# Low terms of gathered quads and of chunks subtracted tile by tile in a one-core graph layer kernel

## The reference

```
h = xn
for layer in range(6):
    agg = segment_sum(h[src], dst, num_segments=n)     # 100000 rows gathered and summed
    z = (h + agg) @ W1[layer] + b1[layer]
    z = relu(batchnorm(z))
    z = z @ W2[layer] + b2[layer]
    h = batchnorm(z)                                   # relu after all layers but the last
x = x + h + mix(xn)
x = x + ffn(layernorm(x))                              # eight experts, two hidden matmuls each
```

## Time and profile before

| | |
|---|---|
| median of 3 runs | 4800.57 us (4792.5 to 4800.67) |
| profiled execution, its own time | 4799.28 us |
| its span | 4797.5 us |
| TensorE busy | 4435.0 us, 92% |
| GpSimd busy | 3121.9 us, 65% |
| VectorE busy | 3031.1 us, 63% |
| ScalarE busy | 2665.6 us, 56% |
| mean granted TensorE clock | 0.962 of full speed |

### The profile page before, as it was taken

How to read it: one execution, slowest core, us unless ns; L and a number is a source line. 1 busy time by engine, 2 the same in 40 slices (tenths; PEclk the granted TensorE clock), 3 DMA queues, 4 the chain that set the end, 5 groups by cost and what they waited for, 6 DMA issues and landing times.

```text
span 4797.5 us, 67657 instructions
## 1 busy us (share of the span) xinstructions
PE 4435.0 (92%) x18799; PEld 3238.3 (68%) x18799; DVE 3031.1 (63%) x6880; ACT 2665.6 (56%) x3373; POOL 3121.9 (65%) x3415
## 2 busy tenths in 40 slices
PE   4999999899988999899988999889998899999999
PEld 3666788587756777477764777567784856666665
DVE  7788766466664666566665666646565566666666
ACT  5667433565536665466545655366554255555555
POOL 5777764077762777457772777627774077877886
PEclk7999999999999999999998999999999899999999
DMA  6444653255533554255543555335545100000000
GB/s 224 155 157 139 209 155 91 79 167 166 155 98 122 171 167 145 58 189 167 158 125 104 165 166 152 98 123 171 165 144 179 39 10 9 9 8 9 8 8 8
DMA packets 197167, 560.26 MB, mean 117 GB/s; under 512 B 44306, under 2 KB 63228, under 8 KB 196668
## 3 DMA queue, kind: packets, MB, share of 16 engines
q0 software_dynamic: 109728, 299.78, 21.3%
q1 hardware_dynamic: 79676, 227.39, 13.9%
q10 hardware_dynamic: 7392, 28.90, 1.5%
HBM read 481.66 MB, written 74.24 MB: 116 GB/s over the span
## 4 chain that ended last, share of the span: by engine, by line
PE 66%; POOL 10%; issue 9%; DVE 6%; DMA 5%; ACT 3%; ACTq 0%; DVEq 0%; POOLq 0%; SPq 0%
PE bank L998 24%; PE bank L1172 11%; PE bank L1181 6%; PE bank L1074 6%; PE bank L903 5%; POOL BIG L737 5%; POOL G L737 5%; PE bank L900 4%; PE bank L946 3%; PE bank L1027 3%; DMA G<-y_table,idx 2%; DMA BIG<-y_table,idx 2%; ACT Gsp L1250 1%; DVE BIG L1506 1%; DVE onehot L1528 1%
## 5 line engine op out<-in xcount | busy, mean ns | idle before, releaser
L737 POOL DMA_INDIRECT G<-y_table,idx x1416 | 1450.1, 1024 | 989.1 <-DMA y_table<-BIG 504.2
L998 PE MATMUL bank<-Ac,Ych 128*128 128x512 f32 x7644 | 1829.9, 393 | 19.3 <-DVE Ych L1512 19.0
L998 PEld LDWEIGHTS bank<-Ac,Ych 128*128 128x128 f32 x7644 | 1447.4, 189 | 328.3 <-DVE Ych L1512 20.2
L1263 ACT CAST Ac<-BIG 128x2048 fp32r<-128x2048 uint8 (+1 forms) x546 | 912.9, 1687 | 373.1 <-PE bank L903 248.2
L737 POOL DMA_INDIRECT BIG<-y_table,idx x870 | 897.7, 1032 | 265.2 <-issue 251.8
L1528 DVE TENSOR_SCALAR onehot<-iota,rel 128x128 fp32r<-128x128 f32 x2290 | 541.5, 306 | 204.2 <-PE bank L903 175.6
L2007 DVE TENSOR_TENSOR G<-G,bank 128x448 f32<-128x448 f32 x784 | 462.1, 619 | 215.2 <-ACT G L1427 112.1
L903 PE MATMUL bank<-Gsp,onehot 128*128 128x512 f32 x1750 | 514.3, 415 | 20.9 <-DVE Gsp L1519 20.7
L1519 DVE TENSOR_TENSOR Gsp<-G,Gsp 128x1024 fp32r<-128x1024 f32 (+1 forms) x230 | 271.0, 1178 | 351.2 <-ACT Gsp L1250 350.9
L1642 DVE TENSOR_TENSOR Z<-Z,bank 128x512 f32 x546 | 374.1, 685 | 185.9 <-PE bank L998 139.3
L1432 ACT ACTIVATE G<-G,fsh,fsc 128x448 f32<-128x448 f32 x448 | 334.0, 757 | 250.9 <-DVE G L2007 245.5
(11 more groups left out here) (226 smaller groups left out, 5354.2 us busy)
## 6 DMA issues: line engine op xcount, KB each, us to landing
BIG<-adjacency SPq DMA_DIRECT2D x273, 448.0 KB, 3.5
BIG<-y_table SPq DMA_DIRECT2D x27, 896.0 KB, 6.5
G<-y_table,idx POOLq DMA_INDIRECT x1416, 2.9
y_table<-BIG SPq DMA_DIRECT2D x25, 896.0 KB, 3.8
adjacency<-BIG ACTq DMA_DIRECT2D x7, 3136.0 KB, 12.9
BIG<-y_table,idx POOLq DMA_INDIRECT x870
BIG<-in_x SPq DMA_DIRECT2D x14, 896.0 KB, 7.4
y_table<-BIG ACTq DMA_DIRECT2D x7, 896.0 KB, 3.7
```

Source lines behind the costliest of these rows:

```text
L737: nc.gpsimd.indirect_dma_start(out=rows[:, j, :], out_offset=None, in_=y_table, in_offset=bass.IndirectOffsetOnAxis(ap=idx[:, t:t + 1], ax ...
L998: last = mm(bank[2 * (k % 2) + b][:, 0:UW], Ych[pos % 2][:, i, s, b * P:(b + 1) * P], Ac[x_ % NAC][:, i - CA * h, :], start=(i == 0 and s ...
L1263: nc.scalar.copy(Ac[x_ % NAC][:, 0:t1 - t0, :], Land[k % NL][:, t0:t1, :]).then_inc(s_ac, 1)
```

## The change

Each low-term subtraction becomes one operation per tile, of 256 columns. The semaphore goes up with the last of them, and the wait stays ahead of the first.

```
             def low_terms(l, pos):

                 dve.wait_ge(s_sh, l * NC + pos + 1)
-                tt(Ych[pos % 2][:, :, 1, :], Rb[row_buffer(pos)], Ych[pos % 2][:, :, 0, :].bitcast(fp32),
-                   ALU.subtract).then_inc(s_sl, 1)
+                for i in range(CT):
+                    last = tt(Ych[pos % 2][:, i, 1, :], Rb[row_buffer(pos)][:, i, :],
+                              Ych[pos % 2][:, i, 0, :].bitcast(fp32), ALU.subtract)
+                last.then_inc(s_sl, 1)

             def quad_low(l, n):

                 dve.wait_ge(s_gh, (l - 1) * N1 + n + 1)
-                m = tiles(n)
-                tt(Gsp[n % RQ][:, 0:m, 1, :], gathered(l, n)[0][:, 0:m, :], Gsp[n % RQ][:, 0:m, 0, :].bitcast(fp32),
-                   ALU.subtract).then_inc(s_gl, 1)
+                for j in range(tiles(n)):
+                    last = tt(Gsp[n % RQ][:, j, 1, :], gathered(l, n)[0][:, j, :],
+                              Gsp[n % RQ][:, j, 0, :].bitcast(fp32), ALU.subtract)
+                last.then_inc(s_gl, 1)
```

## The result

The changed kernel takes 4725.84 us in the median of 4 runs (4723.02 to 4728.22), the kernel before 4797.10 us in 4 (4792.50 to 4800.67): ratio 0.9852, 95% interval 0.9835 to 0.9869, 71 us or 1.5% faster. The forecast was 4727. The profiled execution took 4724.45 us, its span is 4722.7 us.

What follows compares the result with a forecast made beforehand. GpSimd's gathers, stalled 146 us by VectorE's two-input subtractions, were taken to bound the kernel. 4799 less 76 us of stalls plus 3 us of cost gave 4726, adjusted to 4727 for the runs' median; 8-in-10 range 4695 to 4782 us.

Steps and rivals of the forecast that it cites:

- What sets the pace: Gather stages of layers 1 to 5: GpSimd, issuing 350 gathers a layer, sets the pace; stretches sum to 2358.3 us.
- waits for L903 of over 10 us a layer: Sign of TensorE becoming the bound in the dense parts: GpSimd waiting for L903 by over 10 us a layer.
- The stalls: Gathers starting during a two-input VectorE subtraction stand still until it lets go: 146 us before, 70 after the change.
- the factor for where starts fall: Measured stalls over the random-start sum: 0.58 before (146 of 251 us); after, 70 of 79 taken, nearer the random sum.
- One-hots: VectorE's 1750 one-hots, holding the port some 0.14 us each: 13 us of gather stalls before and after.
- So yes: Between two VectorE pieces that follow at once, a waiting gather gets in; inferred from two places in the trace.
- gathers of over 2 us would be gone: Sign in GpSimd's gathers: none over 2 us left, the mean falling from 1.031 to about 0.99 us.
- Does all of it reach the end?: GpSimd's 76 us gain counted whole, since TensorE has 139 us idle in the dense parts and tails.
- TensorE's idle time should have fallen by about 75 us: Sign in dense parts and tails: TensorE's summed idle time falls by about 75 us.
- Rival 1: TensorE becomes the bound in dense parts, so half the gain arrives: 4757 us; chance 0.16, shared with a weaker handover.
- The cost: VectorE runs 1547 more operations, 94 us extra, hidden under its waits for ScalarE except 3 us.
- The start of a layer: TensorE waits 3.65 us for the first chunk's low terms; pieces add 0.38 us a layer, uncovered.

Runs made afterwards that it cites:

- light kernels: Four kernels multiplying 2 of 7 tiles of each dense block; low terms whole 4727.18 us, 256-column pieces 4637.38, one input 4582.72, 128-column pieces 4683.13.
- light one-input kernel: 2 of 7 dense tiles multiplied, low-term subtraction replaced by a whole one-input row copy: 4582.72 us, against 4727.18 with the whole subtraction.
- light kernel before: The kernel before with only 2 of the 7 tiles of each dense block multiplied on TensorE: 4727.18 us against 4799.27.
- two one-input kernels: Kernel before with the subtraction replaced by a one-input row copy, whole or in 256-column pieces: 5238.03 and 5254.19 us against 5240.16.
- one-input kernel: Kernel before with the subtraction replaced by a whole one-input row copy: ratios to it 0.9996, 1.0029 and 1.0021 on three chips.

## Why the prediction was right

**What sets the pace.** Right. The gain is that of GpSimd's stretches, 73 of 75 us. The light kernels show it by experiment, the slow chips by its absence: where GpSimd waits for TensorE, relief of the stalls is worth nothing. The sign that was given against it, waits for L903 of over 10 us a layer, did appear (70.1 us, 14 a layer) and was ill set: it held in the kernel before too (54.5 us, 11 a layer), since 0.30 us of each such wait stands ahead of any gather. Without that, the stretches have 25 us of waits before and 32 after.

**The stalls.** 146 us before, 70 forecast, 69 measured (1724.65 less 1750 times 0.946), inside the bounds 46 and 79. The number was partly lucky in its parts. Without the missed handovers it would have been 54: the factor for where starts fall was nearer to 0.68 than to the 0.9 that I took, and the 15 us of missed handovers were in no sum. One-hots were put at 13 us in both sums; in the light one-input kernel, where little else could stall a gather, all stalls are 2 us.

**"So yes": does a waiting gather get in?** Mostly right, wrong as a rule: 18 in 301 did not, and at 128 columns 61 in 480, for up to 3 us. The forecast that gathers of over 2 us would be gone failed by this, for 4 gathers.

**Does all of it reach the end?** Of 79 us on GpSimd 73 did, the rest went into longer waits for TensorE. The sign that I gave for it was mis-sized: TensorE's idle time should have fallen by about 75 us, and fell by 42 in the dense parts and 9 in the tails. The rest is in its busy time, 1938.4 to 1921.95 and 323.6 to 319.05 us for as many matmuls. The mean granted clock of the run rose from 0.962 to 0.970. That TensorE, with fewer pauses, ran more of its work at the upper of its two levels fits this, and fits the light kernels, where it is busy less (596 of 940 us in the first two stretches of the light kernel before) and the stretches have a granted clock of 0.78 to 0.83; it was not tried by itself, and I had no term for it. The dense parts gave 58 of 71 us. Rival 1's premise, that they have little to give, was true (17 us of idle time are left), but it was just enough.

**The cost.** VectorE's busy time rose from 3031.1 to 3135.8 us, 105 where 94 were forecast. Four pieces take 1.43 us in the record, so one follows another after (1.43 - 0.42)/3 = 0.34, not 0.33: four take 1.35 us where 1.32 were forecast, 13 us over 420 quads, and that is the difference. It was covered: its waits for ScalarE ahead of the low terms fell from 603 to 312 us, and TensorE's wait for them did not rise (20.7 to 18.9). The start of a layer cost what was said: L998's wait for the chunk's low terms rose from 19.0 to 21.0 us in five layers. The Trainium skill ("VectorE: DVE Perf Modes", "The TRN2 errata — SBUF-src ops pay a fixed extra latency per instruction") says that many small tiles pay per tile what a large one pays once, and advises at least 512 elements. That pieces cost VectorE time agrees with this case (105 us more busy time for 1547 more operations), but the advice was no guide to the kernel's time here. On one slow chip, where the two one-input kernels differ by 16 us, it was.

## What to carry to other kernels

When an engine that issues gathers sets the pace, look for gathers that are longer than the shortest, and for what another engine began before them; the remedy may be to cut up an operation of an engine that nobody waits for. Give the operation one input if that can be done, since that removed all but 2 of 144 us of stalls where pieces of 256 columns removed 60%. Don't cut without end: whether the waiting engine gets in between two pieces has to be measured, and with pieces of 128 columns it failed more often than with 256. And check which engine has the pace on the chip at hand: on another chip the same change gained nothing, and on two more neither a half of it nor the one-input kernel did.

## What was not expected of the hardware

- The same program took 4797 to 4799 us on two occasions and 5240, 5269 and 5263 us on three other chips, with late signals from TensorE in the traces of the other kernels that ran there. The gain of 1.5% is that of the first kind; on the one chip of the second kind where the whole change ran it is a loss of 0.3%.
- A missed handover is not a matter of where in the piece a gather begins alone. At 0.07 us into four pieces one stood still for 1.22 us, while others that began as early lost some 0.2. What decides is open.
- The operation that stalls a gather lets it go 0.12 to 0.13 us before its own recorded end, in all 256 stalls by low terms of the kernel before. Nine gathers that began at most 0.04 us after the subtraction were not stalled at all, and a subtraction that begins after the gather's start neither stalls it nor is stalled (353 of 1024 columns begin inside a gather; none took over 1.26 us).
